# Two attention and two feed-forward layers on one core: part of the FP4 weight preparation runs one step later

## The chip, the cores and the metric

The kernel runs on one NeuronCore of a Trainium2 chip. The metric is the time of one launch on the device in microseconds. Durations of single instructions come from one profiled execution.

## The reference

The input `x` has 4 batches of 1024 rows of 256 numbers, all float32. Four layers follow one another, each adding to `x`:

```
x = x + attention0(layernorm(x), ctx)      # 16 heads of 16; keys and values: 77 rows of ctx per batch
x = x + ffn_sine(layernorm(x))             # 256 -> 1024 -> 256, a sine term and relu between
x = x + attention1(layernorm(x), ctx)      # the same form, with a mask
x = x + ffn_fp4(layernorm(x))              # gate and up 256 -> 704, silu(gate) * up, down 704 -> 256
```

In `ffn_fp4` every linear layer first quantizes its input and its weight: in blocks of 16 numbers, `scale = max(|block|) / 6`, each number divided by the scale is rounded to the nearest of 0, 0.5, 1, 1.5, 2, 3, 4, 6 with its sign, and multiplied by the scale again. The weights `w_gate`, `w_up` (704 x 256) and `w_down` (256 x 704) are the same for all rows, so they are quantized once.

## The kernel before

The 4096 rows of `x` lie in SBUF as 32 tiles of 128 rows for the whole program. The program is three blocks: the first attention (`attention` with l = 0), `ffn_sine`, and the second attention (l = 1) together with `Fp4`, whose own loop follows. The change is in the two attentions.

**The attention loop.** One step `i` works on several tiles at once, a software pipeline written out by hand. Every engine has its own `step(i, u)`, its instructions run in that order, and semaphores tie the engines together. In step `i` TensorE computes the scores of tile `i` (L784; in the second attention four mask matmuls, L777, come first), transposes the normalised tile `i + 1` (L793 into `psQ`), transposes the attention output of tile `i - 2` (L793 into `psY`, in `attended`, which waits for `on_ready` and `x_done`), transposes the probabilities of tile `i - 1` (L840), makes the queries of tile `i + 1` (L801) and the output projection of tile `i - 2` (L810), and last multiplies probabilities by values for tile `i - 1` (L868 into `psO`).

VectorE in step `i`: `outputs(i - 2)`, a reciprocal (L498) and a multiply (L501) that read `psO` and write `on`; four row maxima (L507) and four subtractions (L515) on the scores of tile `i`, with L550 for the projection between them; `bn_stats` (L569) of tile `i + 3`; the low part of the queries of tile `i + 1` (L577), for which the next step's scores wait; `normalise` (L530); `bn_aggr` (L589); and `residual` (L525). GpSimd turns the variance of tile `i + 3` into a reciprocal deviation (L665, L667) and adds a bias row to `x` (L674). ScalarE copies and does the exponentials.

**The weight pieces.** The FP4 weights, 4608 columns of `w4`, are quantized in 24 pieces of 192 columns, 12 in each attention. `piece_of(i)` gives a piece for i = 5, 7, ..., 27 (`ATT_LOOP_FROM` = 5, every second step), and None for the rest. The text calls steps with a piece odd and those between even. In an odd step a piece takes four small stages on VectorE (`w4_scales`: L376, L380, L383 with L384, L388) between the other instructions; then one pass on GpSimd, first in its step (`w4_scale_up`, L395); then two passes on VectorE at the end of its step (`w4_powers`, L403 and L406); then three passes on GpSimd at the end of its step (`w4_rounding`, L413, L415, L419). Their buffers `w4scale`, `w4val` and `w4pow` are double, by piece number.

From step 24 of the second attention on, a first part of the FP4 layer's own step (`tail_step`) follows each attention step: on VectorE a `bn_stats` and a `bn_aggr` (L1328, L1335). The transposes of the quantized weights come at step 32 and wait for `w4_done` of all 24 pieces.

Of the kernel before, what the change touches and what calls it, by code (L numbers as in the profile page):

```python
# [58 lines left out]
def wait(eng, sem, count):  # L59

    if not isinstance(count, int) or count > 0:
        eng.wait_ge(sem, count)
# [305 lines left out]
def by_block(ap):  # L368
    return ap.rearrange("p (b q) -> p b q", q=QB)
# [29 lines left out]
def w4_powers(nc, dve, g, n, u):  # L399

    w = g["w4pow"][:, u, :]
    dve.wait_ge(g["w4_val"], n + 1)
    nc.vector.tensor_scalar(w.bitcast(I32), g["w4val"][:, u, :].bitcast(I32), 0x7F800000, 0x00400000, ALU.bitwise_and,  # L403
                            ALU.bitwise_or).then_inc(g["w4_exp"], 1)
    dve.wait_ge(g["w4_exp"], n + 1)
    nc.vector.tensor_scalar(w, w, 1.5, 2.0 ** 22, ALU.max, ALU.mult).then_inc(g["w4_pow"], 1)  # L406


def w4_rounding(nc, pool, g, n, u):

    val, w, neg = g["w4val"][:, u, :], g["w4pow"][:, u, :], g["w4scale"][:, u, 2, :]
    pool.wait_ge(g["w4_pow"], n + 1)
    nc.gpsimd.tensor_tensor(val, w, val, ALU.add).then_inc(g["w4_sum"], 1)  # L413
    pool.wait_ge(g["w4_sum"], n + 1)
    nc.gpsimd.tensor_tensor(val, w, val, ALU.subtract).then_inc(g["w4_round"], 1)  # L415
    pool.wait_ge(g["w4_round"], n + 1)

    piece = by_block(g["w4"][:, bass.ds((n + 1) * PIECE - PIECE, PIECE)])
    nc.gpsimd.tensor_tensor(piece, by_block(val), neg.unsqueeze(2).broadcast_to([P, PB, QB]), ALU.mult  # L419
                            ).then_inc(g["w4_done"], 1)  # L420


def attention(nc, sem, l, g, tail=None):
# [5 lines left out]
    with ExitStack() as ctx:  # L429
# [46 lines left out]
        def piece_of(i):  # L476

            n = i - LOOP_FROM
            return l * (W4_PIECES // 2) + n // 2 if LOOP_FROM <= i < LOOP_TO and n % 2 == 0 else None
# [11 lines left out]
        with nc.Block() as block:  # L491
            @block.vector
            def _(dve):
# [17 lines left out]
                def shift(t, u, j):  # L511
                    wait(dve, mx_set, NB * t + j + 1)
                    if j == 0:
                        wait(dve, prob_mm, 3 * (t - 1))
                    nc.vector.tensor_tensor(  # L515
                        shifted[:, u, 0:HK].rearrange("p (c j n k) -> p j c n k", c=KC, j=NB, n=PAIR)[:, j],
                        psS[j][:, 0:BH * KV].rearrange("p (c n k) -> p c n k", c=KC, n=PAIR),
                        mx[:, u, j * BH:(j + 1) * BH].rearrange("p (c n) -> p c n", c=KC).unsqueeze(3)
                        .broadcast_to([P, KC, PAIR, KV]),
                        ALU.subtract).then_inc(shifted_ready, 1)  # L520
# [12 lines left out]
                def step(i, u):  # L533
                    v = 1 - u
                    if valid(i - 2):
                        outputs(i - 2, u)
                    if tail and i == T:
                        tail_pads()
                        for n in range(2):
                            weight_low(n)  # L540
                    if tail and i == T + 1:
                        tail_step(-1)
                    if valid(i):
                        row_max(i, u, 0)
                        row_max(i, u, 1)
                        shift(i, u, 0)
                    if valid(i - 2):

                        wait(dve, oT_high, i - 1)
                        nc.vector.tensor_tensor(oTs[:, u, 1, :], psY[:, 0:KC * P], oTs[:, u, 0, :].bitcast(F32),  # L550
                                                ALU.subtract).then_inc(oT_low, 1)
                    if valid(i):
                        row_max(i, u, 2)
                        shift(i, u, 1)
                        row_max(i, u, 3)
                        shift(i, u, 2)
                        shift(i, u, 3)
                    if piece_of(i) is not None:
                        if piece_of(i) == 0:
                            dve.wait_ge(g["in_w4"], 16)  # L560
                        w4_scales(nc, dve, g, piece_of(i), piece_of(i) % 2, 0)
                    if l == 0 and i + 3 == 0:
                        dve.wait_ge(g["in_xa"], 16)
                    if l == 0 and i + 3 == 2:
                        dve.wait_ge(g["in_x0"], 16)
                    if l == 0 and i + 3 == R:
                        dve.wait_ge(g["in_x"], 16 * (B - 1))
                    if valid(i + 3):
                        nc.vector.bn_stats(st[:, v, :], x[:, i + 3, :]).then_inc(st_set, 1)  # L569
                        wait(dve, st_set, i + 4)  # L570
                    if piece_of(i) is not None:
                        w4_scales(nc, dve, g, piece_of(i), piece_of(i) % 2, 1)
                    if valid(i + 1):

                        wait(dve, q_high, i + 2)
                        for k in range(KC):
                            last = nc.vector.scalar_tensor_tensor(  # L577
                                qTs[:, v, 1, k, :], psQ[:, k * P:(k + 1) * P],
                                cols[:, C_BQ + 2 * l + k:C_BQ + 2 * l + k + 1], qTs[:, v, 0, k, :].bitcast(F32),
                                ALU.add, ALU.subtract)  # L580
                        last.then_inc(q_low, 1)
                    if piece_of(i) is not None:
                        w4_scales(nc, dve, g, piece_of(i), piece_of(i) % 2, 2)
                    if valid(i + 2):
                        normalise(i + 2, u)
                    if piece_of(i) is not None:
                        w4_scales(nc, dve, g, piece_of(i), piece_of(i) % 2, 3)
                    if valid(i + 3):
                        nc.vector.bn_aggr(mv[:, v, :], st[:, v, :]).then_inc(mv_ready, 1)  # L589
                    for n in quarters_of(i):  # L590
                        w_low_parts(nc, dve, g, n)
                    if valid(i - 2):
                        residual(i - 2)
                    if tail and i == T:
                        for n in range(2, tail.LOWS):
                            weight_low(n)
                    if piece_of(i) is not None:
                        w4_powers(nc, dve, g, piece_of(i), piece_of(i) % 2)

                if tail:  # L600
                    tail_begin, tail_pads, tail_step, weight_low = tail.vector(dve)
                    tail_begin()
# [53 lines left out]
            @block.gpsimd  # L656
            def _(pool):
                def step(i, u):
                    t = i + 3
                    if piece_of(i) is not None:  # L660
                        w4_scale_up(nc, pool, g, piece_of(i), piece_of(i) % 2)
                    if valid(t):
                        v = 1 - u
                        wait(pool, mv_ready, t + 1)
                        nc.gpsimd.tensor_tensor(rstd[:, v, :], mv[:, v, 1:2], expo[:, 1:2], ALU.add).then_inc(ve_set, 1)  # L665
                        wait(pool, ve_set, t + 1)
                        nc.gpsimd.tensor_tensor(rstd[:, v, :], rstd[:, v, :], expo[:, 0:1], ALU.pow  # L667
                                                ).then_inc(rstd_ready, 1)
                    if valid(t - 1):

                        wait(pool, xhat_ready, t)
                        if t == 1:
                            pool.wait_ge(context.bias_done, l + 1)
                        nc.gpsimd.tensor_tensor(x[:, t - 1, :], x[:, t - 1, :], rows[:, ROW, :], ALU.add  # L674
                                                ).then_inc(bias_added, 1)
                    if piece_of(i) is not None:
                        w4_rounding(nc, pool, g, piece_of(i), piece_of(i) % 2)

                if inputs:
                    inputs.fill(pool)  # L680
                if tail:
                    tail_step = tail.gpsimd(pool)
                for i in range(FIRST, LAST):
                    step(i, i % 2)
                    if tail and tail.FIRST <= i - T - 2:
                        tail_step(i - T - 2)
                if tail:
                    for i in range(0, tail.LAST):
                        tail_step(i)
# [956 lines left out]
```

## Time and profile before

| | us |
|---|---|
| median of 3 runs | 993.87 |
| lowest and highest | 991.68, 995.29 |
| the profiled execution | 987.04 |
| its span, first to last instruction | 985.2 |
| busy: TensorE matmul, VectorE, GpSimd | 912.7, 830.7, 465.8 |

The span is cut by the start times of the stages: the first attention has its loop from 17.5 to about 254, the second from 483.6 to about 729, and the FP4 loop fills the rest. A row of the profile names the engine (PE is TensorE's matmul, PEld its weight load, DVE is VectorE, ACT ScalarE, POOL GpSimd), the source line, what is written and read, the shape, and in brackets how long the engine stood idle before and what released it. Instructions of one engine overlap a little at their ends, so the next can start before the one in front of it is shown as ended.

### The profile page before, as it was taken

The page shows a single profiled execution, that of the slowest core. Times are in us where ns is not written, and L with a number is a line of the kernel's source. Part 1 is how long each engine was busy: PE and PEld are TensorE (multiplying, and loading weights), DVE is VectorE, ACT ScalarE, POOL GpSimd, SP SyncE. Part 2 cuts the span into 40 slices and gives each one's busy share as a digit, 9 for nine tenths or more (in the row PEclk, how much of TensorE's full clock was granted, in tenths as well). Part 3 has the DMA queues.
Part 4 walks back from the last instruction along what each step waited for, and adds up shares of the span by engine and source line. Part 5 has one row for each costly group of instructions (what it writes and reads, how often), then busy time and mean ns, then how long its engine had stood idle before and what let it go on. Part 6 is the DMA issues. An engine that isn't in the chain of part 4 may idle for free. (4 is left out here: it accounts for less than half of the span.)

```text
span 985.2 us, 20329 instructions
## 1 busy us (share of the span) xinstructions
PE 912.7 (93%) x7332; PEld 806.9 (82%) x7332; DVE 830.7 (84%) x2172; ACT 485.3 (49%) x1019; POOL 465.8 (47%) x663
## 2 busy tenths in 40 slices
PE   6999999999589999999799999999987999999996
PEld 4889998898478888888689889898876888888885
DVE  5799999997499999998588888899868889889874
ACT  2453443433188787788244333343454444544442
POOL 2233334331266666664322332433247777777662
PEclk9799999999799999999999999999999999999999
DMA  9020000000000000000100000000000000000000
GB/s 341 34 98 2 2 2 1 2 3 1 1 1 1 1 1 1 1 1 1 53 2 2 2 2 2 1 2 2 1 1 1 22 23 1 22 23 22 23 22 22
DMA packets 6083, 18.32 MB, mean 19 GB/s; under 512 B 864, under 2 KB 2784, under 8 KB 5472
## 3 DMA queue, kind: packets, MB, share of 16 engines
q1 hardware_dynamic: 5264, 16.52, 4.4%
q8 instruction: 59, 0.97, 0.4%
q10 hardware_dynamic: 720, 0.50, 0.2%
q14 instruction: 40, 0.33, 0.1%
HBM read 12.83 MB, written 4.19 MB: 17 GB/s over the span
## 5 line engine op out<-in xcount | busy, mean ns | idle before, releaser
L868 PE MATMUL a_psO<-vblk,a_prob 128*128 128x51 f32 (+1 forms) x1280 | 150.0, 273 | 0.0
L868 PEld LDWEIGHTS a_psO<-vblk,a_prob 128*128 128x128 f32 x1280 | 149.6, 194 | 0.0
L1513 PE MATMUL f_psGU<-wgu,f_xTs 128*128 128x512 f32 (+1 forms) x576 | 138.5, 385 | 3.1 <-ACT f_silu L1463 3.1
L507 DVE TENSOR_REDUCE a_mx<-a_psS 128x4 f32<-128x308 f32 x256 | 115.1, 470 | 17.4 <-PE a_psS L784 15.8
L704 ACT COPY a_xTs<-a_psQ 128x256 f32<-128x256 f32 x64 | 23.8, 372 | 206.8 <-PE a_psQ L793 206.8
L715 ACT ACTIVATE a_prob<-a_psT 128x512 f32<-128x512 f32 (+1 forms) x192 | 101.0, 526 | 40.8 <-PE a_psT L840 39.3
L1513 PEld LDWEIGHTS f_psGU<-wgu,f_xTs 128*128 128x128 f32 x576 | 101.9, 189 | 17.7 <-DVE f_xTs L1258 3.4
L840 PE MATMUL a_psT<-ident,a_shifted 128*128 128x128 f32 x640 | 106.3, 281 | 10.8 <-ACT a_prob L715 7.9
L515 DVE TENSOR_TENSOR a_shifted<-a_psS,a_mx 128x308 f32<-128x308 f32 x256 | 114.6, 469 | 0.0
L1095 PEld LDWEIGHTS s_psY<-w,s_hid 128*128 128x128 f32 x768 | 99.4, 188 | 16.6 <-POOL s_hid L1013 12.2
L1095 PE MATMUL s_psY<-w,s_hid 128*128 128x256 f32 x768 | 104.0, 284 | 5.6 <-POOL s_hid L1013 4.9
L1013 POOL TENSOR_TENSOR s_hid<-wat,s_hid 128x512 fp32r<-128x512 f32 x64 | 86.0, 1345 | 39.2 <-ACT wat L1050 39.1
L1083 PE MATMUL s_psH<-s_xTs,w 128*128 128x512 f32 x384 | 102.1, 403 | 2.7 <-DVE s_xTs L994 2.0
L840 PEld LDWEIGHTS a_psT<-ident,a_shifted 128*128 128x128 f32 x640 | 72.7, 142 | 25.0 <-ACT a_prob L715 25.0
L1533 PE MATMUL f_psY<-wdT,f_hTs 128*128 128x256 f32 x384 | 88.3, 379 | 1.6 <-ACT f_hTs L1468 1.6
L1533 PEld LDWEIGHTS f_psY<-wdT,f_hTs 128*128 128x128 f32 x384 | 72.6, 190 | 13.0 <-issue 1.5
L665 POOL TENSOR_TENSOR a_rstd<-a_mv,expo 128x1 f32<-128x1 f32 x64 | 15.2, 238 | 142.9 <-DVE a_mv L589 142.9
L1083 PEld LDWEIGHTS s_psH<-s_xTs,w 128*128 128x128 f32 x384 | 69.2, 192 | 15.5 <-DVE s_xTs L994 2.4
L395 POOL TENSOR_TENSOR w4val<-w,w4scale 128x192 f32<-128x192 f32 x24 | 12.3, 511 | 140.6 <-DVE w4scale L388 140.6
L801 PE MATMUL a_psQ<-a_xTs,wat 128*128 128x128 f32 x512 | 72.4, 285 | 1.9 <-ACT a_xTs L704 1.8
L801 PEld LDWEIGHTS a_psQ<-a_xTs,wat 128*128 128x128 f32 x512 | 63.0, 194 | 5.2 <-ACT a_xTs L704 3.3
L987 DVE TENSOR_SCALAR s_turn<-s_arg 128x512 f32<-128x512 f32 x64 | 51.7, 808 | 14.7 <-ACT s_arg L1063 13.5
(157 smaller groups left out, 1912.8 us busy)
## 6 DMA issues: line engine op xcount, KB each, us to landing
out_x<-x SPq DMA_DIRECT2D x8, 512.0 KB, 2.6
x<-in_x SPq DMA_DIRECT2D x3, 1024.0 KB, 12.8
w<-in_w SPq DMA_DIRECT2D x1, 2304.0 KB, 9.1
w<-in_w SPq DMA_DIRECT2D x2, 1024.0 KB, 17.6
a_mask<-in_mask SPq DMA_DIRECT2D x4, 308.0 KB, 4.0
wat<-in_att SPq DMA_DIRECT2D x1, 1024.0 KB, 22.4
x<-in_x SPq DMA_DIRECT2D x1, 768.0 KB, 9.5
wat<-in_att SPq DMA_DIRECT2D x2, 256.0 KB, 5.5
```

The source lines that it names most:

```text
L507: nc.vector.tensor_reduce(mx[:, u, j * BH:(j + 1) * BH], psS[j][:, 0:BH * KV].rearrange("p (h k) -> p h k", k=KV), AX.X, ALU.max).then_inc ...
L515: nc.vector.tensor_tensor(shifted[:, u, 0:HK].rearrange("p (c j n k) -> p j c n k", c=KC, j=NB, n=PAIR)[:, j], psS[j][:, 0:BH * KV].rearra ...
L715: nc.scalar.activation(prob[:, v, c0 * P:c1 * P], psT[:, 0:(c1 - c0) * P], ACT.Exp, scale=scale).then_inc(prob_ready, 1)
L801: mm = nc.tensor.matmul(psQ[:, h * P:(h + 1) * P], wat[:, k, h * P:(h + 1) * P], xTs[:, u, k * P:(k + 1) * P], start=(k == 0), stop=(k == ...
L840: mm = nc.tensor.transpose(psT[:, (c - c0) * P:(c - c0 + 1) * P], shifted[:, v, c * P:(c + 1) * P], ident[:])
L868: mm = nc.tensor.matmul(psO[:, CH[c] * VW:(CH[c] + n) * VW], prob[:, v, c * P:(c + 1) * P], vblk[:, t // R, c * NJ * VW:(c * NJ + n) * VW] ...
L987: nc.vector.tensor_scalar(k, a, MAGIC, MAGIC, ALU.add, ALU.subtract).then_inc(turn_set, 1)
L1013: nc.gpsimd.tensor_tensor(hid[:, f % 4, 1, :], full[:, f % 2, :], hid[:, f % 4, 0, :].bitcast(F32), ALU.subtract).then_inc(hid_low, 1)
L1083: mm = nc.tensor.matmul(psH[f2 % 4][:], w1[:, a, k, f2 * P:(f2 + 1) * P], xTs[:, u if f + AHEAD < NF else 1 - u, b, k, :], start=(m == 0), ...
L1095: mm = nc.tensor.matmul(psY[q // 2][:, q % 2, :], hid[:, f0 % 4, a, q * P:(q + 1) * P], w2[:, b, f0, :], start=(f0 == 0 and q % 2 == 0 and ...
L1513: mm = nc.tensor.matmul(psGU[:, n0:n1], xTs[:, u, a, k * P:(k + 1) * P], wgu[:, b, k, n0:n1], start=(n == 0), stop=(n == len(TERMS) - 1))
L1533: mm = nc.tensor.matmul(psY[:, 0:D], hTs[:, 1 - u, c * P:(c + 1) * P], wdT[:, c, :], start=(c == 0), stop=(c == NF1 - 1))
```

## The change

The last two stages of a piece move from the odd step to the even step behind it. On VectorE the two power passes no longer stand at the end of the odd step, behind `residual`; they stand in the middle of the next step, behind the last of the subtractions on the scores and ahead of `bn_stats`. On GpSimd the three rounding passes stand at the end of the next step, where before they stood at the end of the odd step. Nothing is added or taken away; the number of instructions and their shapes are the same.

```diff
@@ vector step(i, u)
                         row_max(i, u, 3)
                         shift(i, u, 2)
                         shift(i, u, 3)
+                    if piece_of(i - 1) is not None:
+                        w4_powers(nc, dve, g, piece_of(i - 1), piece_of(i - 1) % 2)
                     if piece_of(i) is not None:
                         if piece_of(i) == 0:
                             dve.wait_ge(g["in_w4"], 16)
...
                     if tail and i == T:
                         for n in range(2, tail.LOWS):
                             weight_low(n)
-                    if piece_of(i) is not None:
-                        w4_powers(nc, dve, g, piece_of(i), piece_of(i) % 2)
-
@@ gpsimd step(i, u)
-                    if piece_of(i) is not None:
-                        w4_rounding(nc, pool, g, piece_of(i), piece_of(i) % 2)
+                    if piece_of(i - 1) is not None:
+                        w4_rounding(nc, pool, g, piece_of(i - 1), piece_of(i - 1) % 2)
```

## Rows read from the trace of the kernel before

**Rows 1.** The page, busy time of TensorE over the span.

```profile
PE 912.7 (93%) x7332; PEld 806.9 (82%) x7332; DVE 830.7 (84%) x2172; ACT 485.3 (49%) x1019; POOL 465.8 (47%) x663
```

**Rows 2.** Busy time by window, cut where a step's first score matmul starts.

```profile
core 0: us, PE busy (x) PEld busy (x) DVE busy (x) ACT busy (x) POOL busy (x), PEclk, DMA share, GB/s
68.56:225.96 157.40, 152.88 (x1659) 141.98 (x1658) 144.81 (x471) 64.17 (x161) 58.91 (x119) 1.00 0.01 2
225.96:232.58 6.62, 6.56 (x75) 6.19 (x74) 5.35 (x15) 2.74 (x7) 1.57 (x3) 1.00 0.01 2
508.77:666.26 157.49, 156.26 (x1674) 141.53 (x1674) 139.12 (x448) 61.12 (x156) 53.19 (x107) 1.00 0.01 2
666.26:673.43 7.17, 7.11 (x79) 6.43 (x78) 6.40 (x23) 2.74 (x7) 1.03 (x3) 1.00 0.01 2
673.43:681.00 7.57, 7.26 (x79) 6.41 (x79) 7.17 (x23) 2.84 (x7) 3.92 (x9) 1.00 0.00 0
```

**Rows 3.** Waits from 75.64 to 225.96 us: total, times, longest.

```profile
PE a_psY L793 <- DVE a_on L501: 3.1, 11, 0.4
DVE w4pow L403 <- POOL w4val L395: 2.6, 11, 0.2
```

**Rows 4.** Timeline of TensorE, first attention, steps 23 and 24.

```profile
185.00 0.90 PE L784 MATMUL a_psS<-a_kblk,a_qTs 32*128 32x154 f32 x24
...
186.10 0.38 PE L793 MATMUL a_psY<-ident,a_on 128*128 128x128 f32 x2
...
191.61 0.90 PE L784 MATMUL a_psS<-a_kblk,a_qTs 32*128 32x154 f32 x24
...
193.16 0.44 PE L793 MATMUL a_psY<-ident,a_on 128*128 128x128 f32 x2 [0.27 <-DVE a_on L501]
...
198.65 0.90 PE L784 MATMUL a_psS<-a_kblk,a_qTs 32*128 32x154 f32 x24
```

**Rows 5.** Timeline of VectorE, the same steps.

```profile
185.93 0.86 DVE L507 TENSOR_REDUCE a_mx<-a_psS 128x4 f32<-128x308 f32 x2
...
191.29 0.39 DVE L525 TENSOR_TENSOR x<-x,a_psY 128x256 f32<-128x256 f32 x1
191.92 0.26 DVE L403 TENSOR_SCALAR w4pow<-w4val 128x192 int32<-128x192 int32 x1 [0.23 <-POOL w4val L395]
...
192.39 0.25 DVE L498 RECIPROCAL a_rden<-a_psO 128x16 f32<-128x16 f32 x1
...
193.02 0.85 DVE L507 TENSOR_REDUCE a_mx<-a_psS 128x4 f32<-128x308 f32 x2
...
195.66 0.85 DVE L515 TENSOR_TENSOR a_shifted<-a_psS,a_mx 128x308 f32<-128x308 f32 x2
...
196.88 0.61 DVE L577 SCALAR_TENSOR_TENSOR a_qTs<-a_psQ,cols,a_qTs 128x128 fp32r<-128x128 f32 x2
...
197.82 0.39 DVE L525 TENSOR_TENSOR x<-x,a_psY 128x256 f32<-128x256 f32 x1
198.76 0.26 DVE L498 RECIPROCAL a_rden<-a_psO 128x16 f32<-128x16 f32 x1 [0.55 <-PE a_psO L868]
```

**Rows 6.** Timeline of GpSimd, the same steps.

```profile
193.32 0.59 POOL L413 TENSOR_TENSOR w4val<-w4pow,w4val 128x192 f32<-128x192 f32 x1
...
194.66 0.51 POOL L419 TENSOR_TENSOR w<-w4val,w4scale 128x192 f32<-128x192 f32 x1
197.98 0.19 POOL L665 TENSOR_TENSOR a_rstd<-a_mv,expo 128x1 f32<-128x1 f32 x1 [2.82 <-DVE a_mv L589]
...
198.77 0.73 POOL L674 TENSOR_TENSOR x<-x,rows 128x256 f32<-128x256 f32 x1
```

**Rows 7.** Timeline of VectorE, second attention, steps 25 and 26.

```profile
667.84 0.86 DVE L507 TENSOR_REDUCE a_mx<-a_psS 128x4 f32<-128x308 f32 x2 [0.65 <-PE a_psS L784]
...
674.30 0.42 DVE L1328 BATCH_NORM_STATS2 f_st<-x 128x6 f32<-128x256 f32 x1
...
674.86 0.22 DVE L498 RECIPROCAL a_rden<-a_psO 128x16 f32<-128x16 f32 x1
```

**Rows 8.** Timeline of TensorE, second attention, step 26.

```profile
675.60 0.44 PE L793 MATMUL a_psY<-ident,a_on 128*128 128x128 f32 x2 [0.27 <-DVE a_on L501]
```

## The prediction

> **What bounds the kernel now.** I read the page first: TensorE is busy for 93% of the span, the most of all engines [rows 1], so a gap on TensorE is what counts. Then the windows [rows 2]. Steps 6 to 28 of the first attention take 157.40 us for 23 steps; step 29, in which no piece is in hand, takes 6.62. If all were like it, the 23 would take 152.26: 5.14 us are lost somewhere. In the second attention steps 3 to 24 take 157.49 for 22, 7.16 each, and step 25 with its piece 7.17, all at a granted clock of 1.00 and with TensorE busy 99% of the time; step 26 takes 7.57.
>
> The waits say where the 5.14 are [rows 3]: 11 times in 22 steps TensorE waits for `on` (L501) before it transposes it (L793). The timeline gives the place [rows 4]. In odd step 23 the scores start at 185.00 and the transposes of `on` at 186.10, 1.10 behind, with no wait. In even step 24 the scores start at 191.61 and the transposes at 193.16, 1.55 behind, after a wait. So the even step is 7.04 long (191.61 to 198.65) and the odd one 6.61. The difference of 0.43 is the lateness of `on`.
>
> VectorE's rows tell why `on` is late [rows 5]. At the end of the odd step `residual` starts at 191.29. Behind it stand the two power passes, the first held for 0.23 by GpSimd's scale-up, starting at 191.92. The reciprocal of the next step, the first half of `on`, starts only at 192.39. Without the passes it starts 0.11 behind the scores, as at 198.76 against 198.65: at 191.72.
>
> **What the change does, part by part.** *Removed from the step boundary:* the wait for `w4val` and two passes, 192.39 - 191.72 = 0.67 us of lateness of the reciprocal. VectorE itself is ready by then: the instruction behind a `residual` can start some 0.30 behind its start (an estimate from the overlaps of these rows), so at 191.59, and the 191.72 is TensorE's. Of the 0.67 TensorE feels only the 0.43 computed above, since until 1.10 behind the scores it has other work. So an even step of the first attention goes from 7.04 to 6.62. The gain can't be larger than that, as 6.62 is what the steps take that have no piece or an odd piece, with TensorE busy 6.56 of it [rows 2]; the lower bound is nothing. I take the whole: 12 even steps (6, 8, ..., 28) x 0.42 = 5.0 us. The remaining 0.1 of the 5.14 belongs to single longer steps, and I leave it.
>
> *Second attention, steps up to 25:* the even steps already take the odd ones' 7.16, because four more matmuls stand ahead of the scores and TensorE comes to `on` later. The waits of that stretch have no row for `on`. Gain 0.
>
> *Second attention, steps 26 and 28:* from step 24 on the FP4 layer's two statistics instructions follow, too. They start at 674.30, and the reciprocal at 674.86, so they cost 0.56 [rows 7]. With the power passes in front the reciprocal comes 1.43 behind the step's start (673.43), and TensorE waits for `on` at 675.60 [rows 8]: the step takes 7.57 [rows 2]. That is 0.41 over 7.16, and by the position in the order step 28 has the same. TensorE needs `on` at 675.60 - 0.41 = 675.19 and has it 0.74 behind the reciprocal's start (675.60 - 674.86), so the reciprocal may start up to 1.02 behind the step's start. After the change the odd step's VectorE queue runs as follows. Its row maxima start 1.58 behind the step's start (667.84 against 666.26, where they wait for the scores). From row maxima to the end of `residual` an odd step takes 191.59 - 185.93 = 5.66. The statistics take 0.56. Together 7.80, which is 0.64 into the next step, under 1.02. Gain 2 x 0.41 = 0.8 us.
>
> *Added in the middle of the even step:* two power passes cost from the first start to the next instruction's 192.39 - 191.92 = 0.47 (their wait is gone: GpSimd's scale-up ended over 4 us before). All VectorE work behind them in the step comes 0.47 later, and each has its cover. (a) The queries' low part ends at 197.49 against 193.02 for the row maxima, 4.47 later; the maxima start 0.93 behind the scores (185.93 against 185.00), so it ends at 5.40, now 5.87, and the next scores want it at 6.62: 0.75 left. (b) `residual` can be left 5.10 behind the maxima (197.82 + 0.30 - 193.02), so at 0.93 + 5.10 + 0.47 = 6.50 behind the scores; the next reciprocal is released at 6.62 + 0.11 = 6.73: 0.23 left. (c) In the odd step the same sum is 0.93 + 5.66 = 6.59, 0.14 left. This is the tightest, and it does not change. In the second attention (b) is 1.58 + 5.57 = 7.15 of 7.16, and with the statistics 7.71, 0.55 into the next step against the 1.02 allowed. So the added part costs 0. Uncovered it would be 0.47 x 24 = 11.3 us. What the pair costs in its new place I bound by 0.36 (two passes less their overlaps of about 0.08) and 0.7 (both durations and a release of 0.15); only above 0.47 + 0.23 does anything come later, and only above 0.9 would TensorE of the first attention wait, since the reciprocal may be 0.33 late there (1.10 - 0.77, as 193.16 is 0.77 behind 192.39).
>
> *GpSimd:* the three rounding passes run from 193.32 to 195.17, then it idles 2.82 until the next statistics [rows 6]. In the new place they stand behind the bias add, from about 199.5 to 201.4, the same phase one step later. What is queued behind them is the next scale-up, which waits for VectorE until some 6 us into the odd step, so nobody waits for them; they themselves wait for nothing, as the power passes end some 3 us before. No DMA is issued by any moved instruction, and none is moved past. The last piece is done at step 28 in place of 27, and its reader is step 32.
>
> The row shows a power pass of 192 columns in 0.26 us, the reduction over the same columns in 0.34. The Trainium skill (SBUF — State Buffer, section "Who interferes with whom") says that a VectorE pass in a two-port mode, which its copy and tensor_scalar forms can enter, and a GpSimd instruction shut each other out for the whole instruction. By that rule the order would matter: before, the second pass lay beside GpSimd's power instruction; in the new place GpSimd is idle, so by the rule too the sum stays. Its rival is the fourth below.
>
> **Sum.** 5.0 + 0.8 = 5.8 us. Against the profiled execution's 987.04 that is 981.2. The median of the runs shown is 993.87, 0.7% above it; the gain is a count of gaps and not a share, so I take it off the median: 988.0 us, 0.6% faster. About 0.3%, 3 us, is what a measurement of this kernel can tell from no change.
>
> **Rivals.**
>
> 1. *Forecast:* both gains, 988.0, with 987.5 to 989.0 as its own range. For it: steps without the passes in both attentions take exactly the short time. Chance 0.80.
>
> 2. *VectorE becomes the bound of the first attention.* Its odd step has only 0.14 us of slack, its even step only 0.23. If the pair costs its upper bound, or the reciprocal is released later than I read, each even step keeps part of the delay. With half of the gain left: 993.87 - 2.5 - 0.8 = 990.6; with a quarter, 991.8. Against it: TensorE itself allows 0.33 more. Chance 0.10.
>
> 3. *The change does nothing:* the stall returns as another wait at once, for instance because 0.43 of lateness hides a wait of equal length for the projection's transposes. Time 993.9. Against it: in odd steps, with the same TensorE order, nothing of the kind shows. Chance 0.06.
>
> 4. *The slower side: the moved passes collide and land on the path.* Place: the middle of the even step in both attentions. If a power pass and a GpSimd pass (0.59) excluded each other there, or VectorE reached the queries' low part over 0.75 late, the scores of the odd step would wait. It decides from a price of the pair of 0.47 + 0.75 = 1.22 in the first attention. At 0.47 + 2 x 0.59 = 1.65 the scores come 0.43 late, and the first attention is where it was; in the second VectorE's queue would end at 7.15 + 1.18 = 8.33, so the reciprocal comes 1.17 into the next step against the 1.02 allowed: 12 x 0.15 = 1.8. If the odd steps, whose queue is tighter still, lose as much again: 993.87 + 3.6 = 997.5. Against it: GpSimd's 2.82 idle at that place. Chance 0.04.
>
> **How the numbers follow.** Faster by over 0.3% (below 990.9): the forecast and about half of rival 2, 0.84. Within: the rest of 2, and 3, 0.12. Slower: rival 4, 0.04. The range of 8 in 10 holds the forecast's own and rival 2's, with the scatter of a median (the three runs spread over 3.6 us): 985.8 to 991.4.
>
> **What would show it.** Windows: even steps of the first attention at 6.62 like the odd ones, steps 26 and 28 of the second at 7.16. Waits: no row for `on` (L793 after L501) in the loop of either attention, and none for `w4val` ahead of L403. Timeline: the power passes right behind L515, the reciprocal 0.11 behind the scores in both kinds of step; the low part of the queries 0.7 ahead of the next scores. It would be wrong if a wait of TensorE for L577 showed, if VectorE's idle time ahead of L498 were gone and `on` still late, or if the median fell by under 3 us although the windows show the gaps closed.

## The result, and the profile after

The changed kernel takes 986.38 us (median of 20 runs), the kernel before 992.9 beside it (20 runs). The ratio is 0.9936, 95% interval 0.9919 to 0.9954: 6.4 us or 0.64% faster (the medians differ by 6.5), against the 5.8 us forecast.

The profile shows it in the windows. These are the changed kernel's, with the columns of [rows 2]: steps 6 to 28 of the first attention, steps 3 to 28 of the second, then steps 25, 26 and 27 of the second.

```profile
68.63:220.84 152.21, 150.92 (x1657) 142.32 (x1656) 145.86 (x471) 63.00 (x161) 56.89 (x115) 1.00 0.01 2
510.92:697.04 186.12, 184.68 (x1979) 167.26 (x1979) 165.87 (x536) 72.07 (x184) 61.23 (x123) 1.00 0.01 2
668.39:675.56 7.17, 7.11 (x79) 6.44 (x79) 6.72 (x25) 2.74 (x7) 3.08 (x7) 1.00 0.01 2
675.56:682.70 7.14, 7.08 (x78) 6.42 (x78) 6.77 (x23) 2.74 (x7) 1.91 (x5) 1.00 0.00 0
682.70:689.87 7.17, 7.11 (x78) 6.44 (x78) 6.72 (x25) 2.74 (x7) 3.09 (x7) 1.00 0.02 3
```

The first line answers to 157.40 in [rows 2]: 5.19 us less for 23 steps, 6.62 each. Step 26 of the second attention takes 7.14 in place of 7.57. The whole stretch 186.12 answers to 186.96 before (157.49 + 7.17 + 7.57 from [rows 2], and 7.16 + 7.57 for steps 27 and 28): 0.84 less. Together the loops give 6.0 us.

These are the waits of the changed kernel, 75 to 225 us, all six rows. Neither row of [rows 3] is left: TensorE (PE) waits for nothing that the view shows, its weight loads (PEld) only for ScalarE, and VectorE (DVE) has no row.

```profile
ACT a_xTs L703 <- PE a_psQ L792: 68.4, 23, 3.0
POOL a_rstd L664 <- DVE a_mv L591: 55.4, 12, 4.6
POOL w4val L395 <- DVE w4scale L388: 36.4, 11, 3.4
ACT a_prob L714 <- PE a_psT L839: 11.6, 22, 0.5
ACT a_qTs L721 <- PE a_psQ L800: 8.5, 23, 0.4
PEld a_psT L839 <- ACT a_prob L714: 6.0, 23, 0.3
```

The timeline of VectorE from the end of odd step 23 to the start of step 25, to be read beside [rows 5]:

```profile
187.44 0.38 DVE L525 TENSOR_TENSOR x<-x,a_psY 128x256 f32<-128x256 f32 x1
187.86 0.26 DVE L498 RECIPROCAL a_rden<-a_psO 128x16 f32<-128x16 f32 x1
...
192.11 0.25 DVE L403 TENSOR_SCALAR w4pow<-w4val 128x192 int32<-128x192 int32 x1
192.39 0.26 DVE L406 TENSOR_SCALAR w4pow<-w4pow 128x192 f32<-128x192 f32 x1
192.57 0.42 DVE L571 BATCH_NORM_STATS2 a_st<-x 128x6 f32<-128x256 f32 x1
...
193.96 0.39 DVE L525 TENSOR_TENSOR x<-x,a_psY 128x256 f32<-128x256 f32 x1
194.48 0.26 DVE L498 RECIPROCAL a_rden<-a_psO 128x16 f32<-128x16 f32 x1
```

and TensorE's starts of steps 24 and 25 with the transposes of `on`, beside [rows 4]:

```profile
187.75 0.90 PE L783 MATMUL a_psS<-a_kblk,a_qTs 32*128 32x154 f32 x24
...
188.86 0.38 PE L792 MATMUL a_psY<-ident,a_on 128*128 128x128 f32 x2
...
194.37 0.90 PE L783 MATMUL a_psS<-a_kblk,a_qTs 32*128 32x154 f32 x24
```

The reciprocal stands 0.11 behind the scores in both steps, the transposes of `on` 1.11 behind them with no wait. The power passes lie in the even step's middle and cost 192.57 - 192.11 = 0.46, from their start to the start of the next instruction.

GpSimd (POOL) in the same stretch, beside [rows 6]:

```profile
194.12 0.19 POOL L664 TENSOR_TENSOR a_rstd<-a_mv,expo 128x1 f32<-128x1 f32 x1 [4.63 <-DVE a_mv L591]
...
194.91 0.72 POOL L673 TENSOR_TENSOR x<-x,rows 128x256 f32<-128x256 f32 x1
195.59 0.60 POOL L413 TENSOR_TENSOR w4val<-w4pow,w4val 128x192 f32<-128x192 f32 x1
```

It is idle from 189.5 to 194.12, and the power passes at 192.11 to 192.65 fall into that gap. The experiments show that this matters.

### The profile page after: what moved, and what is told of

It is laid out like the page before. It is cut to its first block and busy times, and to the rows that moved or that the text cites. A ratio compares the mean times of both kernels' runs of the same rounds, so it can differ in the third digit from the quotient of the medians.

```text
span 987.9 us, 20329 instructions
## 1 busy us (share of the span) xinstructions
PE 920.6 (93%) x7332; PEld 816.5 (83%) x7332; DVE 831.9 (84%) x2172; ACT 484.2 (49%) x1019; POOL 465.8 (47%) x663
## 5 line engine op out<-in xcount | busy, mean ns | idle before, releaser
L867 PE MATMUL a_psO<-vblk,a_prob 128*128 128x51 f32 (+1 forms) x1280 | 152.1, 275 | 0.0
L867 PEld LDWEIGHTS a_psO<-vblk,a_prob 128*128 128x128 f32 x1280 | 151.8, 196 | 0.0
L809 PE MATMUL a_psY<-a_wo,a_oTs 128*128 128x256 f32 x384 | 63.1, 301 | 1.6 <-DVE a_oTs L550 1.6
```

The source lines that it names most:

```text
L809: mm = nc.tensor.matmul(psY[:, 0:D], oTs[:, u, a, k * P:(k + 1) * P], wo[:, b, k, :], start=(m == 0), stop=(m == len(terms) - 1))
L867: mm = nc.tensor.matmul(psO[:, CH[c] * VW:(CH[c] + n) * VW], prob[:, v, c * P:(c + 1) * P], vblk[:, t // R, c * NJ * VW:(c * NJ + n) * VW] ...
```

## The experiments

All run on one core with the same inputs. The last two columns are window lengths in each run's one profiled execution: first attention, steps 6 to 28, and second attention, steps 3 to 28.

| kernel | ratio to before, 95% interval | first, us | second, us |
|---|---|---|---|
| before | | 157.40 | 186.96 |
| changed | 0.9936 (0.9919 to 0.9954) | 152.21 | 186.12 |
| rounding_only | 1.0011 (0.9984 to 1.0039) | 157.40 | 186.92 |
| powers_only | 0.9945 (0.9909 to 0.9981) | 152.20 | 186.10 |
| boundary | 0.9996 (0.9966 to 1.0027) | 157.40 | 186.28 |
| late_boundary | 0.9977 (0.9943 to 1.0011) | 154.89 | 186.61 |
| behind_outputs | 0.9955 (0.993 to 0.998) | 152.84 | 186.18 |
| narrow_bias | one run, 987.36 us | 152.31 | 186.26 |
| extra1 | 0.9949 (0.9913 to 0.9985) | 152.20 | 186.09 |
| extra2 | one run, 998.01 us | 160.63 | 191.99 |
| coef_late | 0.9934 (0.9907 to 0.996) | 152.22 | 186.12 |

The windows of two executions of one kernel agree within 0.02 us, where the times of single runs spread over some 10. So the verdicts below go by steps and waits.

**rounding_only: which half of the change counts.**

```diff
 kernel before, gpsimd step
-                    if piece_of(i) is not None:
-                        w4_rounding(nc, pool, g, piece_of(i), piece_of(i) % 2)
+                    if piece_of(i - 1) is not None:
+                        w4_rounding(nc, pool, g, piece_of(i - 1), piece_of(i - 1) % 2)
```

> Only the three rounding passes on GpSimd move to the even step; the power passes stay at the end of VectorE's odd step behind the wait for the scale-up. Theory: even steps of the first attention stay at 7.04, steps 26 and 28 of the second at 7.57, and the time is that of before within 0.3%. Rival (part of the gain is GpSimd's, because its rounding no longer lies beside the even step's row maxima and subtractions): even steps get shorter by more than 0.1 us.

Measured: 157.40, even steps 7.04 as before, steps 26 and 28 of the second attention 7.57. GpSimd's half alone gives nothing; the rival is out.

**powers_only: the other half alone.**

```diff
 changed kernel, gpsimd step
-                    if piece_of(i - 1) is not None:
-                        w4_rounding(nc, pool, g, piece_of(i - 1), piece_of(i - 1) % 2)
+                    if piece_of(i) is not None:
+                        w4_rounding(nc, pool, g, piece_of(i), piece_of(i) % 2)
```

> Only the two power passes on VectorE move to the even step; the three rounding passes stay at the end of GpSimd's odd step, where they now wait for the powers. Theory: the gain is VectorE's alone. Even steps of the first attention take 6.62 us, steps 26 and 28 of the second 7.16, as in the changed kernel; rounding runs right behind the powers and its end, some 0.4 us behind where the next statistics (L665) would start, keeps nobody waiting. 5.8 us faster than before. Rival, a collision: the rounding passes (0.59 each) now run beside VectorE's normalise (L530, 0.40), and if the two engines shut each other out there, normalise takes up to 1.0, the queue leaves the even step at 6.50 + 0.59 = 7.09, the reciprocal comes 0.47 into the odd step against the 0.33 allowed, and 12 odd steps get 0.14 longer: 1.7 us less gain.

Measured: 152.20 and 186.10, both windows of the changed kernel. VectorE's half is the whole gain in them. Two things came besides. First, the collision of the rival is real but smaller than it was priced. VectorE's `normalise` (L530) in powers_only, and GpSimd's second rounding pass beside it:

```profile
195.45 0.59 DVE L530 TENSOR_SCALAR a_xhat<-x,a_mv,a_rstd 128x256 f32<-128x256 f32 x1
```

```profile
195.30 0.59 POOL L415 TENSOR_TENSOR w4val<-w4pow,w4val 128x192 f32<-128x192 f32 x1
```

It takes 0.59 in place of 0.41. The 0.2 stay under the 0.23 of slack at the step's end: the next reciprocal is still 0.11 behind the scores. Second, behind the windows, step 29 of the second attention took 7.85 in place of 7.14 to 7.17. The waits of 508 to 700 us name it:

```profile
POOL w4val L413 <- DVE w4pow L406: 45.3, 12, 3.8
...
PEld a_psY L792 <- DVE a_on L501: 0.8, 1, 0.8
DVE f_shift L1299 <- POOL f_rstd L1397: 0.8, 1, 0.8
```

GpSimd stands at L413 for up to 3.8 us, and with it the FP4 layer's first deviations (L1397) queued behind. VectorE wants them once, at the end of step 28, and `on` is late by it. So the expected "keeps nobody waiting" was wrong at this one place, and moving the rounding passes too is worth 0.7 us there. That is by the steps; the times of the two kernels (0.9945 and 0.9936) can't be told apart.

**boundary and late_boundary: is it the wait or the passes?**

```diff
 boundary: changed kernel, vector step(i, u)
                     v = 1 - u
+                    if piece_of(i - 1) is not None:
+                        w4_powers(nc, dve, g, piece_of(i - 1), piece_of(i - 1) % 2)
                     if valid(i - 2):
                         outputs(i - 2, u)
 (and no longer behind shift(i, u, 3))
```

> As the changed kernel, but the two power passes stand first in the even step, ahead of the reciprocal, and no longer in its middle. So the wait for GpSimd is gone and the passes still stand ahead of the output of the step. Theory (lateness adds up in the queue): VectorE is free 6.59 behind the start of the odd step, 0.03 ahead of the next, the pair costs 0.47, so the reciprocal comes 0.44 into the even step against the 0.33 allowed: even steps of the first attention 6.73, steps 26 and 28 of the second 7.80 + 0.47 - 7.16 = 1.11 against 1.02, so 7.25. Gain over before 12 x 0.31 + 2 x 0.32 = 4.4 us. Rival (the wait for GpSimd is all of it): even steps 6.62, gain 5.8. Rival (the place is all of it): 7.04 less the wait of 0.23, gain 3.1 us or less.

Measured: 157.40, every even step of the first attention as long as before; no gain. I had the edit wrong. In the first attention nothing stands on VectorE between the end of one step and the start of the next, so the order is the same as before, wait included. VectorE in boundary:

```profile
190.63 0.26 DVE L403 TENSOR_SCALAR w4pow<-w4val 128x192 int32<-128x192 int32 x1 [0.23 <-POOL w4val L395]
190.93 0.26 DVE L406 TENSOR_SCALAR w4pow<-w4pow 128x192 f32<-128x192 f32 x1
191.10 0.25 DVE L498 RECIPROCAL a_rden<-a_psO 128x16 f32<-128x16 f32 x1
```

In steps 26 and 28 of the second attention the two statistics instructions stand between and fill the wait; the same instructions as before stand ahead of the reciprocal. There the steps took 7.24, as expected (7.25): of the 0.41 over 7.16, 0.33 went with the wait and 0.08 stayed for the passes. For the first attention the question was put again:

```diff
 late_boundary: changed kernel, vector step(i, u), at the end; GpSimd's rounding likewise
+                    if piece_of(i - 2) is not None:
+                        w4_powers(nc, dve, g, piece_of(i - 2), piece_of(i - 2) % 2)
 w4_scales, part 2, ahead of the reciprocal
+        if n >= 2:
+            dve.wait_ge(g["w4_done"], n - 1)
```

> The run named boundary gave VectorE the same order as the kernel before in the first attention (last in the odd step and first in the even step are the same place), so it took no wait away there. This one does: at the end of an odd step stand the power passes of the piece of the odd step before, whose scale-up ended long ago, and the rounding follows on GpSimd; a wait on work finished two steps earlier is added ahead of L384. Theory (lateness adds up): VectorE free at 6.59, the pair costs 0.47, so the reciprocal comes 0.44 into the even step against the 0.33 allowed; even steps 8 to 28 of the first attention take 6.73, steps 26 and 28 of the second 7.25. Gain over before 12 x 0.31 + 2 x 0.32, about 4.4 us. Rival, the place alone counts: even steps at 7.04, no gain. Rival, the wait alone counts: 6.62, gain 5.8.

Measured: even steps from 8 on 6.84 to 6.87 (one 6.95), 154.89 in all; steps 26 and 28 of the second attention 7.38. Both one-sided rivals are out: with the wait gone 0.23 of the 0.42 per step stays. The expected 6.73 was too short, and the rows of VectorE and GpSimd say why:

```profile
188.09 0.40 DVE L405 TENSOR_SCALAR w4pow<-w4val 128x192 int32<-128x192 int32 x1
188.53 0.26 DVE L408 TENSOR_SCALAR w4pow<-w4pow 128x192 f32<-128x192 f32 x1
188.71 0.25 DVE L500 RECIPROCAL a_rden<-a_psO 128x16 f32<-128x16 f32 x1
```

```profile
187.87 0.51 POOL L397 TENSOR_TENSOR w4val<-w,w4scale 128x192 f32<-128x192 f32 x1 [5.53 <-DVE w4scale L390]
```

The first pass takes 0.40 in place of 0.26 and ends at 188.49, 0.11 behind the end of GpSimd's scale-up of the next piece (188.38), which runs beside it. The pair costs 0.62 in place of 0.47, and the reciprocal comes 0.60 behind the scores (188.11). So 0.15 of what stays is this collision, which the kernel before doesn't have. Without it some 0.1 of the 0.42 would stay for the passes (an estimate, 0.23 less 0.15), much as in the second attention, where 7.38 is 0.14 over the 7.24 of boundary. Most of the loss is the wait, a smaller part the passes.

Three executions give TensorE's allowance. The reciprocal is 0.78 behind the scores in the kernel before, 0.60 in late_boundary and 0.58 in the odd steps of extra2 below, and the steps are 0.42, 0.23 and 0.22 longer. So it may be 0.36 late; the prediction had 0.33.

**behind_outputs and narrow_bias: does any place behind the output do?**

```diff
 behind_outputs: changed kernel, vector step(i, u)
                     if valid(i - 2):
                         outputs(i - 2, u)
+                    if piece_of(i - 1) is not None:
+                        w4_powers(nc, dve, g, piece_of(i - 1), piece_of(i - 1) % 2)
 (and no longer behind shift(i, u, 3))
```

> As the changed kernel, but the two power passes stand right behind L501 and ahead of the first row maximum of the even step. Theory: what counts is only that they stand behind the output on VectorE. The row maxima start at 0.11 + 0.65 + 0.47 = 1.23 behind the scores in place of 0.93, the queue leaves the step at 6.33, L550 ends at 2.8 behind the scores with the projection wanted at 3.09. All steps of the first attention 6.62, steps 26 and 28 of the second 7.16: the time of the changed kernel. Rival: the step is bound by how soon the row maxima follow the scores, since L550 and the subtractions hang on them, and even steps get longer by up to 0.30, 12 x 0.30 = 3.6 us slower than the changed kernel.

Measured: 152.84, ten of the twelve even steps 6.67 to 6.69 (6 and 22 stay at 6.61 and 6.62), and one wait that is new: TensorE's weight loads of the projection for L552 (`oTs`), 10 times, 3.0 us in sum. The rival's path exists. But it opens only because the pair costs 189.68 - 188.65 = 1.03 us there. VectorE, then GpSimd, in behind_outputs:

```profile
188.65 0.25 DVE L403 TENSOR_SCALAR w4pow<-w4val 128x192 int32<-128x192 int32 x1
188.93 0.83 DVE L406 TENSOR_SCALAR w4pow<-w4pow 128x192 f32<-128x192 f32 x1
189.68 0.85 DVE L507 TENSOR_REDUCE a_mx<-a_psS 128x4 f32<-128x308 f32 x2
```

```profile
188.40 0.55 POOL L666 TENSOR_TENSOR a_rstd<-a_rstd,expo 128x1 f32<-128x1 f32 x1
188.92 0.73 POOL L673 TENSOR_TENSOR x<-x,rows 128x256 f32<-128x256 f32 x1
```

L406 takes 0.83 in place of 0.26. It ends at 189.76, again 0.11 behind the GpSimd instruction beside it (189.65). In these ten steps the bias add (L673) starts 0.01 to 0.02 ahead of L406. In steps 6 and 22 L406 starts first, by 0.03 and 0.08, takes its 0.26, and the bias add takes 0.81 and 0.77 in place of 0.73. To test that this is the cause:

```diff
 narrow_bias: behind_outputs, gpsimd step
-    nc.gpsimd.tensor_tensor(x[:, t - 1, :], x[:, t - 1, :], rows[:, ROW, :], ALU.add
+    nc.gpsimd.tensor_tensor(x[:, t - 1, 0:1], x[:, t - 1, 0:1], rows[:, ROW, 0:1], ALU.add
```

> As the run behind_outputs, but GpSimd's bias add (L673) works on one column of x in place of 256, so the bias is left out of the other 255 and the output changes. In behind_outputs the second power pass (L406) took 0.83 us in place of 0.26 and ended 0.11 behind the end of the bias add that ran beside it (188.92 + 0.73). Theory (the two shut each other out): with nothing wide on GpSimd beside it L406 takes 0.26, and the even steps of the first attention go from 6.67 to 6.62. Rival (the pass is slow for its place behind L501, by a dependence or a full queue): L406 stays at 0.8.

Measured: L406 takes 0.260 to 0.295 (median 0.286), even steps 6.62. With the same order on VectorE and no wide instruction beside it the pass is fast, so the collision was the cause. The rival of a slow place is out. The 0.29 fits too: L673 still runs beside L406, now for 0.19 (187.03 to 187.22), and L406 ends at 187.33, again 0.11 behind it.

The Trainium skill (SBUF — State Buffer, section "Who interferes with whom") states that a VectorE instruction in a two-port mode and a GpSimd instruction exclude each other for the whole instruction. The traces agree for the scale-up, the rounding passes and the bias add: 0.40, 0.59 and 0.83 where 0.26, 0.41 and 0.26 are usual. They differ for GpSimd's one-column power instruction: L403 in behind_outputs (188.65 to 188.90) lies wholly within L666 (0.55 us) and takes its usual 0.25. In the kernel before the same holds for L406 (192.21 to 192.47) within L667 (192.11 to 192.66): all 24 take 0.26.

**extra1 and extra2: how much cover is there in the new place?**

```diff
 extra1 (EXTRA = 1), extra2 (EXTRA = 2): changed kernel, ahead of the pair, EXTRA more pairs
                     if piece_of(i - 1) is not None:
+                        dve.wait_ge(g["w4_val"], piece_of(i - 1) + 1)
+                        spare_powers(nc, dve, g, piece_of(i - 1), piece_of(i - 1) % 2)
                         w4_powers(nc, dve, g, piece_of(i - 1), piece_of(i - 1) % 2)
```

`spare_powers` is `w4_powers` with a tile `spare` as its target.

> The changed kernel with one more pair of power passes in the new place, into a spare tile, ahead of the real pair: extra work of 0.47 us on VectorE in each of the 24 even steps; nothing reads it. Theory (the new place has cover): the queue leaves the even step at 6.50 + 0.47 = 6.97, the reciprocal comes 0.35 into the odd step against the 0.33 allowed: pair of steps 13.26 instead of 13.24; second attention unchanged at 7.16, its last even steps just at their limit. 0.3 us slower than the changed kernel. Rival (VectorE's queue is the bound, no cover left): each pair of steps 0.4 to 0.47 longer, 24 x 0.47 = 11 us slower than the changed kernel and 5 slower than before.

Measured: 152.20 and 186.09, nothing lost, and no wait of TensorE in the windows. The reciprocal of the odd step is 0.36 behind the scores (196.21 and 195.85), just at the allowance. 24 more pairs, 11 us of VectorE, cost nothing but 0.06 in step 29 of the second attention (7.22), behind the window. The rival of a VectorE already at its bound (the prediction's second) is out.

> The changed kernel with two more pairs of power passes in the new place: extra work of 0.94 us in each even step. Theory: the queries' low part ends 5.87 + 0.94 = 6.81 behind the scores, past the 6.62 at which TensorE wants it, so TensorE waits for L577's successor line. First attention: even step 6.81, then the reciprocal 0.63 into the odd step, 0.30 late, so 6.92: a pair takes 13.73 against 13.24. Second attention: low part 1.58 + 5.88 = 7.46 against 7.16, even step 7.46, odd 7.16. Slower than the changed kernel by 12 x 0.49 + 12 x 0.30 = 9.5 us. Rival (VectorE alone sets the time once the cover is used up): by its queue alone a pair takes 0.63 + 6.51 + 0.63 + 5.66 = 13.43 in the first attention and stays at 14.32 in the second: 2.3 us slower.

Measured: even steps 6.98 and odd ones 6.84 in the first attention, against 6.81 and 6.92; even steps 7.62 in the second, against 7.46. With one step of 8.41 in a stretch of low clock left out, the first window is 6.9 us longer than in the changed kernel, the second 5.9: 12.7 against 9.5 expected and 2.3 by the rival. The place is as expected. VectorE's row of the queries' low part (L598 here, L577 before) and TensorE's start of the next scores:

```profile
201.97 0.61 DVE L598 SCALAR_TENSOR_TENSOR a_qTs<-a_psQ,cols,a_qTs 128x128 fp32r<-128x128 f32 x2
```

```profile
202.63 0.90 PE L802 MATMUL a_psS<-a_kblk,a_qTs 32*128 32x154 f32 x24 [0.30 <-DVE a_qTs L598]
```

The sizes were short by two terms left out: 0.05 from the end of L598 (202.58) to the start of the scores, and 0.11 for the first spare pair, which waited for its own last pass ahead of the second. The odd steps of the first attention were 0.08 shorter than expected, by the wider allowance.

**coef_late: another late reciprocal.**

```diff
-                    if i == 4 and inputs:
+                    if i == 30 and inputs:
                         inputs.coefficients(dve)
```

> The changed kernel with the five small instructions for the sine layer's coefficients (L335 to L340) issued behind step 30 of the first attention and no longer behind step 4. Theory: step 5 takes 7.13 in the changed kernel for the same reason as the even steps did before, work between residual and the reciprocal; it takes 6.62 without it, and in step 31 VectorE waits more than 1.1 us for TensorE ahead of the reciprocal, which hides the 1.4 us of the five. 0.5 us faster than the changed kernel, 6.3 faster than before. Rival: they land on the path behind step 30 and step 31 gets longer by the same 0.5: no difference.

Measured: step 5 takes 6.62 in place of 7.13. Behind step 30 the five instructions leave VectorE 0.62 of idle time ahead of the next reciprocal where it has 1.44 in the changed kernel, so they are hidden. But the reason that I gave, the work between `residual` and the reciprocal, is the smaller part. VectorE, then GpSimd, in the changed kernel at the end of step 4:

```profile
61.73 0.60 DVE L340 TENSOR_SCALAR thb<-thb 128x8 f32<-128x8 f32 x1
62.36 0.26 DVE L498 RECIPROCAL a_rden<-a_psO 128x16 f32<-128x16 f32 x1
```

```profile
61.57 0.73 POOL L673 TENSOR_TENSOR x<-x,rows 128x256 f32<-128x256 f32 x1
```

The last of the five, on 8 columns, is held by the bias add and takes 0.60; in coef_late and in narrow_bias it takes 0.17. In narrow_bias the five stand where they stood, and step 5 takes 6.70. So 0.43 of the 0.51 is the collision and 0.08 the work. By steps coef_late beats both kernels, 0.5 us under the changed one; by time it can't be told from it (0.9934 against 0.9936).

**before_again and after_again: why the changed kernel's profile had the longer span.**

> The kernel before, once more. The profiled execution of the changed kernel has a longer span (987.9) than that of before (985.2) though its even steps are short; between 240 and 270 us and near 505 us it shows a lower granted clock. Theory: how long the clock is low at the ends of the stages differs from one execution to the next; both kernels show stretches of differing length. The steps: 7.04 again in every even one.

> The changed kernel, once more. Steps again 6.62 and 7.16. If the longer low clock near 245 and 505 us is due to the change, it is there again and the span is again near 988; if it comes by chance, the span falls anywhere from 978 to 988.

Measured: before_again has a span of 991.9 with windows of 157.41 and 186.98; after_again 983.8 with 152.22 and 186.12. The rest of the span, outside these two windows, is 640.8 and 647.5 for the kernel before and 649.6 and 645.5 for the changed one. So the windows repeat to 0.02 us and the rest moves by up to 9 between executions of kernels that are the same there. The clock is part of it. In the 40 us from the first scores of step 31 of the first attention on, TensorE's work thins out and its clock falls for a while to the lower of its two levels (0.50 in windows of 5 us). The mean granted clock of these 40 us is 0.83 and 0.82 in the two executions of the kernel before, 0.66 and 0.70 in the two of the changed one: some 14 and 27 us at the lower level (40 x 2 x 0.17, 40 x 2 x 0.34).

The other traces show that this doesn't come with the short steps. Boundary, with the steps of the kernel before in this attention, has 0.66; powers_only and extra1, with those of the changed kernel, have 0.79. The timed runs agree: the mean granted clock is 0.978 over the 20 of the changed kernel and 0.978 to 0.980 over the 67 of the kernel before that stand beside the experiments. Within each kernel the runs with a lower clock are the longer ones, by 0.5 to 0.9 us for each 0.001. So the clock spreads the times and doesn't make the difference.

A second low stretch of the changed kernel, near 505 us (0.77 over 15 us), makes step 2 of the second attention 10.03 long in place of 7.14. It is absent in after_again. Of the seven executions with short steps in both attentions four have it (changed, extra1, coef_late, narrow_bias), of the other six (the two of the kernel before, rounding_only, boundary, late_boundary, extra2) none. Whether that is chance is not shown.

## Why the prediction was right

*The place of the loss.* The 5.14 us were put down to `on` coming late in 12 even steps, and the change took 5.19 off that stretch. *The first term*, 12 x 0.42 = 5.0, measured 5.19. The 0.1 that I left aside as single longer steps closed too. It was mostly step 22: 7.15 before, 6.62 after. *The second term*, 2 x 0.41 = 0.8 in steps 26 and 28 of the second attention, measured 0.84. The 7.16 of the other steps there did not change, as forecast. *Sum:* 5.8 forecast, 6.0 by the windows, 6.4 by the ratio with an interval of 4.6 to 8.0. What lies between 6.0 and 6.4 is within the scatter and is put down to nothing. The median of 986.38 lies below the forecast's own 987.5 to 989.0, though within the wide range: the 5.8 was taken off the 993.87 of three runs, and off the 992.9 of 20 runs it gives 987.1.

*The cover in the new place.* VectorE is free 0.30 behind the start of `residual` (187.44 and 193.96). The slack at the odd step's end was given as 0.14 and is 187.86 - 187.74 = 0.12; at the even step's as 0.23 and is 194.48 - 194.26 = 0.22. What lies beyond, the 0.33 that TensorE allows, is 0.36 and held in extra1; the edge by the queries' low part held in extra2, 0.16 sooner than worked out.

*The price of the pair.* 0.47 forecast, 0.46 measured. But the upper bound of 0.7 was too low as a bound: the same pair cost 1.03 in behind_outputs. It held here because GpSimd idles at that place, which the prediction named (2.82 idle, [rows 6]) but used only against rival 4. That rival's mechanism is real, its place was wrong. In the changed kernel the pair starts 4.36 behind the even step's start. The collision is at 1.03 in behind_outputs, and at 5.80 in powers_only. The prediction also noted that by the exclusion the second pass, which lay beside GpSimd's power instruction before, should have been slowed there; it took 0.26 there too.

*What the 0.67 was made of.* The prediction took the wait and the two passes off together and didn't ask for the share of each. By boundary and late_boundary most of the loss was the wait.

*GpSimd's part.* "Nobody waits for them" was right for the change as made. What the rounding passes would cost if they had stayed, 0.7 us at step 29, the prediction did not ask.

*Rivals.* 2 (VectorE the bound) fell with extra1, 3 (another wait at once) with the waits of the changed kernel, which show none for TensorE.

## What to carry to other kernels

Work on an engine that is 84% busy can be free, as the extra pair of extra1 was, or lengthen the step, by what stands behind it in the queue. Find the one result that the bounding engine waits for (here `on`), and move everything that isn't needed for it behind it; 0.42 us came back in every second step of the first attention although no instruction went away. When choosing the new place, look at the other engine's timeline too: VectorE's power passes, which read and write SBUF alone, want a gap in GpSimd's wide instructions, and even 8 columns (L340) lost 0.43 beside one. And if a waiting step is moved on one engine, move the step that waits for it on the other too, or what is queued behind it pays.

## What the hardware showed that I had not expected

A power pass of 192 columns takes 0.26 us alone and was held until 0.11 us behind the end of a GpSimd instruction that had started first: to 0.40 in late_boundary and to 0.83 in behind_outputs (medians of 24). In behind_outputs a start 0.01 to 0.02 us behind the other's decided it. GpSimd's one-column power instruction of 0.55 us did not hold it; its one-column add of 0.19 did, to 0.29. Two executions of the same kernel differ by 6.7 us in span (985.2 and 991.9), with the loops equal to 0.02.
